# A decoder layer: the soft mask on VectorE, fill matmuls, four column blocks in cross attention, and expert rows added in DRAM by the scatter

## The reference

```
x = x + attn(layernorm(x))       # 16 heads of 128, in 8 segments of 64 tokens, over 2 batches of 512
x = x + xattn(layernorm(x), ctx) # 16 heads of 16, causal, keys and values from ctx_512
x = x + experts(layernorm(x))    # top 2 of 8 experts
```

## Time and profile before

| | us |
|---|---|
| median of 3 runs | 564.37 |
| the runs | 564.37, 571.93, 560.82 |
| the profiled execution, its own time | 561.27 |
| its span, first to last instruction | 559.5 |
| TensorE busy | 491.8 (88%) |
| VectorE busy | 339.7 (61%) |
| ScalarE busy | 323.3 (58%) |
| POOL busy | 144.0 (26%) |

### The profile page before, as it was taken

How to read it: one execution, slowest core, us unless ns; L and a number is a source line. 1 busy time by engine, 2 the same in 40 slices (tenths; PEclk the granted TensorE clock), 3 DMA queues, 4 the chain that set the end, 5 groups by cost and what they waited for, 6 DMA issues and landing times. The chain is left out here.

```text
span 559.5 us, 11805 instructions
## 1 busy us (share of the span) xinstructions
PE 491.8 (88%) x4163; PEld 419.0 (75%) x4164; DVE 339.7 (61%) x749; ACT 323.3 (58%) x762; POOL 144.0 (26%) x141
## 2 busy tenths in 40 slices
PE   2989999999899999999989799998507999999960
PEld 1778888888898888888689677776405888888850
DVE  5376666666725666666566376666652666666654
ACT  4477777788416777777662388887203444444430
POOL 5110000013000000000000438998011455555530
PEclk9999999999899999999999899999857999999995
DMA  9411111111100112110000033442221344444527
GB/s 264 160 59 57 56 56 56 56 57 57 39 1 20 57 57 56 56 56 0 1 1 2 2 101 127 147 131 102 76 94 51 119 169 156 151 159 158 165 76 225
DMA packets 24001, 48.05 MB, mean 86 GB/s; under 512 B 2960, under 2 KB 11168, under 8 KB 23968
## 3 DMA queue, kind: packets, MB, share of 16 engines
q1 hardware_dynamic: 21120, 41.17, 22.9%
q0 software_dynamic: 2240, 6.04, 3.1%
q10 hardware_dynamic: 608, 0.39, 0.3%
HBM read 42.48 MB, written 5.11 MB: 85 GB/s over the span
## 5 line engine op out<-in xcount | busy, mean ns | idle before, releaser
L651 PE MATMUL psum<-a_xt_hi,a_qk_hi 128*128 128x512 f32 x128 | 54.8, 428 | 1.4 <-DVE a_xt_lo L508 1.4
L570 DVE COPY a_weights_t<-psum 64x256 f32<-64x256 f32 x32 | 13.7, 428 | 63.5 <-PE psum L766 63.5
L1391 POOL DMA_INDIRECT picks_dram<-x_wout,e_pick_row x23 | 38.7, 1683 | 52.3 <-DVE x_wout L1554 52.3
L651 PE MATMUL psum<-a_xt_lo,a_qk_hi 128*128 128x512 f32 x128 | 51.7, 404 | 0.0
L651 PE MATMUL psum<-a_xt_hi,a_qk_lo 128*128 128x512 f32 x128 | 50.8, 397 | 0.0
L967 ACT ACTIVATE x_probs<-psum,x_neg_max 128x128 f32<-128x128 f32 x128 | 45.3, 375 | 8.1 <-DVE x_neg_max L1024 8.1
L1432 ACT ACTIVATE e_inner_hi<-psum 128x512 fp32r<-128x512 f32 x23 | 13.7, 598 | 57.9 <-PE psum L1614 57.9
L896 POOL MEMSET x_mask<- 128x512 bf16 x1 | 0.5, 524 | 172.3 <-POOLq L248 172.3
L1605 PE MATMUL psum<-expert_w_hi,e_x_hi 128*128 x92 | 39.2, 426 | 2.2 <-DVE e_x_lo L1532 2.2
L936 POOL TENSOR_TENSOR expert_w_lo<-x_xn_t,expert_w_hi 128x1024 fp32r<-128x1024 f32 x16 | 37.7, 2355 | 1.3
L780 PE MATMUL psum<-a_weights_t,a_v 64*128 64x64 f32 x256 | 34.9, 276 | 3.4 <-issue 2.5
(11 more groups left out here) (232 smaller groups left out, 1486.3 us busy)
## 6 DMA issues: line engine op xcount, KB each, us to landing
x_k_t<-in_expert_wo SPq DMA_DIRECT2D x23, 512.0 KB
a_qk_raw<-in_wqk SPq DMA_DIRECT2D x32, 256.0 KB, 2.6
x_xn_t<-in_expert_w SPq DMA_DIRECT2D x16, 512.0 KB, 3.8
a_wv_raw<-in_wv SPq DMA_DIRECT2D x17, 256.0 KB, 2.8
x_sb<-in_x SPq DMA_DIRECT2D x2, 512.0 KB, 5.1
x_k_t<-in_wo SPq DMA_DIRECT2D x1, 1024.0 KB, 10.5
x_v<-in_wo SPq DMA_DIRECT2D x1, 1024.0 KB, 13.1
xn_dram<-xn SPq DMA_DIRECT2D x1, 1024.0 KB, 4.4
```

The costliest lines, as they stand in the source:

```text
L570: dve.tensor_copy(weights_t[SEG:P, :, 0:2, :], t_ps[SEG:P, :, 0:2, :]).then_inc(wt_ready, 1)
L651: last = pe.matmul(out, pick_l(left[a], k), pick_r(right[b], k), start=start and n == 0, stop=n == 3 * KD - 1, skip_group_check=not start)
L1391: pool.indirect_dma_start(out=picks_dram, out_offset=bass.IndirectOffsetOnAxis(ap=pick_row[:, tile:tile + 1], axis=0), in_=y_rows[:, slot, ...
```

## The change

In attention:

- The mask is mixed once, into PSUM bank 3, and VectorE copies it to SBUF (`mask_f`). Per head the mask matmul goes; VectorE adds the mask to the scores (one operation more) and takes the maximum from SBUF.
- TensorE gets fill matmuls, whose results nobody reads, of 128x512 in fp32: four before the first transposes, eight behind them, and four in expert_phase while it waits for the first gather. The first transposes go sequence by sequence, each when its own xn is ready.
- The queries and keys of head 17 are made ahead of `output(0)`, and two of the eight cross products ahead of `output(1)`.

In cross attention `weigh` runs once per sequence with 16 matmuls, ordered so that four blocks of 32 partitions come in turn.

In the experts `sums_dram` holds one row per token and begins as a copy of x. The scatter adds into it (`compute_op=ALU.add`); each scatter waits until the one before has landed. So the share must be in y before: 48 small matmuls bring each row's share to its partition (`row_share`), and the copy of y multiplies with it. The tail is four DMAs from `sums_dram` to the output. VectorE's loop over the tiles is unrolled.

```diff
@@ attention
+            dve.wait_ge(mask_mixed, 1)
+            dve.tensor_copy(mask_f[:, :], c.bank[3][:, 0:HB * SEG])
...
-                dve.tensor_reduce(row_max[:, :, :], soft_ps, AX.X, ALU.max).then_inc(max_ready, 1)
+                dve.tensor_tensor(shifted[:, :, :, :].rearrange("p j g t -> p (j g t)"), c.bank[2][:, 0:HB * SEG], mask_f[:, :],
+                                  ALU.add).then_inc(masked_ready, 1)
+                dve.wait_ge(masked_ready, s.n + 1)
+                dve.tensor_reduce(row_max[:, :, :], shifted[:, :, :, :], AX.X, ALU.max).then_inc(max_ready, 1)
...
+            def keep_busy(times):
+                filled = sigma[:, :, :, :].rearrange("p a b t -> p (a b t)")
+                for _ in range(times):
+                    pe.matmul(c.bank[2][:, :], filled[:, 0:P], filled[:, 0:BANK], start=True, stop=True)
...
-                pe.matmul(c.bank[2][:, 0:HB * SEG], mixed_b[:, :], mask[:, :, :], start=True, stop=False,
-                          skip_group_check=True)
...
+            pe.wait_ge(fills_ready, 1)
+            keep_busy(4)
             pe.wait_ge(consts_ready, 6)
-            pe.wait_ge(fills_ready, 1)
+            pe.matmul(c.bank[3][:, 0:HB * SEG], mixed_b[:, :], mask[:, :, :], start=True, stop=True).then_inc(mask_mixed, 1)
             transpose_x(0)
+            keep_busy(8)
...
                 if not s.at(HALVES - 1, H - 1):
                     linear_scores(s.n + 1)
+                if s.at(0, H - 1):
+                    project(s.n + 2, 1, s.member, True)
+                elif s.at(HALVES - 1, H - 1):
+                    cross_products(range(6, 8))
                 if s.at(s.half, H - 1):
                     output(s.half)
@@ cross attention
-                for place, group, k, odd in across_groups(ch):
-                    head = k * CH + group * 2 + odd
-                    last = pe.matmul(ht_ps[group * ROWG:(group + 1) * ROWG, k, :],
-                                     v_pad[:, b % 2, head, :], probs_t[:, ch, place, :],
-                                     start=odd == 0, stop=odd == 1)
+                for k in range(KD):
+                    for odd in range(2):
+                        for group in range(4):
+                            last = pe.matmul(ht_ps[group * ROWG:(group + 1) * ROWG, k, :], v_pad[:, b % 2, k * CH + group * 2 + odd, :],
+                                             probs_t[:, group // 2, (group % 2) * 4 + k * 2 + odd, :], start=odd == 0, stop=odd == 1)
@@ experts
+            sp.dma_start(sums_dram[0:B * P, :].rearrange("(b p) d -> p b d", p=P), c.x_sb[:, :, :]).then_inc(sums_begun, 16)
+            sp.dma_start(sums_dram[B * P:(B + 1) * P, :], c.x_sb[:, 0, :]).then_inc(sums_begun, 16)
...
-            for b in range(B):
-                for k in range(TOPK):
-                    sp.dma_start(picked[k][:, b, :], picks[:, k, b, :]).then_inc(gathered[b], 16)
-            for b in range(B):
-                sp.wait_ge(mixed, TOPK * (b - b % 2) + 3 + b % 2)
-                sp.dma_start(out[b], c.x_sb[:, b, :]).then_inc(out_stored, 16)
+            for b in range(0, B, 2):
+                sp.dma_start(out[b:b + 2].rearrange("b p d -> (b p) d"), sums_dram[b * P:(b + 2) * P, :]).then_inc(out_stored, 16)
...
                 pool.wait_ge(y_ready, tile + 1)
-                pool.indirect_dma_start(out=picks_dram, out_offset=bass.IndirectOffsetOnAxis(ap=pick_row[:, tile:tile + 1], axis=0),
-                                        in_=y_rows[:, slot, :], in_offset=None).then_inc(y_stored[slot], 16)
+                if tile > 0:
+                    pool.wait_ge(y_stored[1 - slot], 16 * ((tile + 1) // 2))
+                pool.indirect_dma_start(out=sums_dram, out_offset=bass.IndirectOffsetOnAxis(ap=sum_row[:, tile:tile + 1], axis=0),
+                                        in_=y_rows[:, slot, :], in_offset=None, compute_op=ALU.add).then_inc(y_stored[slot], 16)
...
-                dve.tensor_copy(y_rows[:, slot, :], y_ps[slot]).then_inc(y_ready, 1)
+                dve.tensor_scalar(y_rows[:, slot, :], y_ps[slot], row_share[:, tile:tile + 1], None, ALU.mult).then_inc(y_ready, 1)
...
             pe.wait_ge(owner_known, 1)
+            for _ in range(4):
+                pe.matmul(c.bank[7][:, :], c.ident[:, :], c.x_sb[:, 0:2, :], start=True, stop=True)
             pe.wait_ge(picks_known, 1)
...
             columns(1, 1, 0, False)
+            pe.wait_ge(in_share_ready, 1)
+            for n in range(PICKS):
+                for part in range(3):
+                    last = pe.matmul(share_ps, row_hot[:, n, :], in_share[:, n, part, :],
+                                     start=n == 0 and part == 0, stop=n == PICKS - 1 and part == 2)
+            last.then_inc(row_share_done, 1)
```

148 lines of the change are left out of this document (79 added, 69 removed).

## The result

| | before | after |
|---|---|---|
| median | 565.5 (4 runs, 560.82 to 571.93) | 569.54 (4 runs, 568.93 to 575.0) |
| profiled execution / its span | 561.27 / 559.5 | 568.93 / 567.1 |
| ratio after / before | | 1.0137, 95% interval 1.0087 to 1.0188 |

The kernel became slower by 0.9 to 1.9%. The forecast was 549, faster by 2.2%; 569.5 lies in the upper part of its range, but on the wrong side of "no change".

A forecast was written before the change was run, and what follows sets the result against it. It took each stage to have its own bound (ScalarE's copy at heads, TensorE among expert tiles, DMA in the tail). Sum: 561.3 + 2.3 + 0 - 2.3 - 1.7 - 5.2 - 2.2 + 2 - 5.5 = 548.7, said 549; range 540 to 572.

The forecast's parts named there:

- the stores: Experts: each adding scatter waits for the landing before, interval 4.95 instead of 4.86 over 22 intervals, +2 us.
- rival (a): Experts, POOL's wait before each store: adding stores become the bound; chance 0.20 above 5.5 us apart, 0.16 above 6.0.
- L: Experts: time from one adding store's issue to the next's, put at 3.14 + 1.54 + 0.27 = 4.95 us.
- sign of being wrong: Experts or heads: store interval above 5.5, or the head's copy of the transposed weights waiting for VectorE.
- The next load, which has 4 us of slack: Experts, POOL: the load of tile+2 queues behind the store's wait and was said to have 4 us of slack.
- Cross attention: -5.2: Cross attention: weighing once instead of twice saves 0.65 us in each of eight batches, -5.2; ends -4 and -7.
- Fills at the start: +2.3: Start of attention: eight fills delay the first product, which then runs at full clock; +2.3 us, from -0.5 to +5.
- The mask: Attention heads: VectorE's added operation is narrowly covered by ScalarE's wait; 0 us in all, from -3 to +3.
- The half change: Between attention halves: head 17's product fills TensorE's wait; -1.5 from order and -0.8 from the clock, -2.3 us.
- The end of attention: Before the output of half 1: two cross products fill TensorE's wait of 2.27; -1.7 us, from 0 to -1.7.
- the fills in the prologue: Start of the experts: four fills during the gather wait raise the clock for tile 0; -2.2 us, chance three in four.
- the tail: End of the kernel: four DRAM-to-DRAM copies replace sixteen loads and the mixes; -5.5 us, from -4 to -7.

The follow-up runs named there:

- the two sum buffers: Kernel before with the experts' part of the change alone, but adding scatters alternate between two buffers without waiting for the one before: 569.14, ratio 1.012.
- the combined kernel: Kernel before plus new order, single weigh with five fills, prologue fills, mask on TensorE, plain scatters and a tail of eight 256 KB loads: 553.87, ratio 0.9837.

## Why the prediction was wrong

**The step that failed: the stores, "+2".** The mechanism was in the forecast as rival (a), with the right place and break-even: L = 5.5 breaks even against the other terms, and L came out at 5.52. Inside L the landing was right (4.68 forecast, 4.75 measured), the hand-over was not: "POOL has such a gap too behind the landing, an estimate of 0.27" took TensorE's issue gaps of 0.20 to 0.33 for POOL's gap behind a landing, which is 0.77. 0.5 x 22 = 11 of the 12.6 missed are this, and the landing's 0.07 x 22 = 1.5 the rest. The forecast stood 0.09 above the interval it had to fit under, so any error in L was multiplied by 22. The forecast's own sign of being wrong, an interval above 5.5, is what came.

That the landing came out right is in part luck. It was put together from an issue beside VectorE (1.71) and a reading priced by one gather, whose 4.24 was long for this stage (those behind it land in 3.4 to 3.9) and ends at the landing, so that the 0.3 for TensorE's start had no place in it. In the chain POOL issues away from VectorE's operation, in 1.59, and the landing follows 3.16 later, where 2.97 was forecast. Beside that operation, as the forecast had it, an adding store's issue takes 2.31 and its landing 6.0 to 6.6 (the two sum buffers).

**"The next load, which has 4 us of slack"** was wrong as well, though in the chained kernel it did not decide. In the kernel before TensorE already waited for the gather at 5 of the tiles from 440 to 540 (1.4 in all), so there was no slack; with two buffers a gather delayed by 0.6 on POOL held it at 16 (8.6).

**"Cross attention: -5.2"** was right for the sequences: a period fell by 0.70, for 0.65 taken, and the -4.5 in the table are the seven periods between the first and the last spread. The column blocks overlap fully: the rule of the Trainium skill ("TensorE: Matmul & The Clock Gate", Part 3: Packing small matmuls, section The mechanism) that a weight load overlaps running matmuls only when the row group differs, which would have had -4, is not borne out by the 1.08 for thirty-two records. The limit was not the one named. ScalarE's waits for the maximum, which should be gone, are still 6.7 of 8.1. Between the first and the last spread TensorE's busy time fell from 56.3 to 49.2, 1.0 per period, and it now waits 2.9 in all for ScalarE's exponentials, for 0.3 before. (The 0.20 behind a go was also counted twice, in the 0.53 and in the 1.0.) What failed is that I let the stage end with its last sequence. In the stretch behind it the faster stage met POOL, whose work has its own pace, and TensorE, less busy than before, lost its clock: +6.2.

**"Fills at the start: +2.3"** came out at +1.9, but fills and mask share it: taken away from the changed kernel the fills give back 1.0, and 0.9 stay, which are the mask's and which I had at 0. **The mask** over the other heads is 0.03 to 0.04 per head less in most steps and 0.45 more in three, together within the ends; in those three the cover was not there. **The half change** (-2.6 for -2.3) has the right sum from parts that were not: the clock, low from 144.1 to 147.5 before and not at all now, gives 1.7 instead of 0.8, and the order 0.9 instead of 1.5. **The end of attention** (-2.2 for -1.7), **the fills in the prologue** (-2.8 for -2.2) and **the tail** (-6.5 for -5.5) were right in mechanism and size.

**The clock drop between heads 1 and 2** (2.9 of the +3.4) was in no case of mine. It stays open what lets it come.

So the rest without the stores was worth 14.6 - 7.6 = 7.0 and not 14.6. The stretch behind cross attention took 6.2 of the difference and the heads 1 and 2 took 3.4; the terms that came out better than forecast gave about 2 back.

## What to carry to other kernels

Before making a stage shorter, look at what runs beside its end at its own pace (here POOL's last split at 388 to 391), and at what TensorE has left to do there: a collision that lay 1 us away cost 1.9, a clock at half behind a TensorE that was less busy 4 more, and the stage had gained 4.5. A chain of DMAs, one behind the other's landing, is priced by landing plus the waiting engine's own gap after a landing, taken from a row of that engine; and where it comes within a tenth of the interval that it must fit, its error is multiplied by the number of links. Taking a bound away (two buffers) needs the next one priced first: here POOL's way to the gather, behind the issue of the adding store.

## What the runs showed of the hardware

- POOL starts its next indirect DMA 0.73 to 0.77 behind the landing that it waited for, with an adding store as with a plain one; behind VectorE's signal 0.28. SP goes on 0.02 behind a landing, ScalarE 0.03 (the combined kernel).
- An adding scatter of 128 KB lands 4.75 after the start of its issue in the chain (median), 3.7 to 3.9 in the last three stores, and 6.0 to 6.6 when it is issued next to VectorE's operation; a plain one lands in 2.40 by itself and 3.15 next to that operation. The issue takes 1.55 by itself and 2.31 next to VectorE's operation, against 0.97 and 1.71.
- Sixteen plain fp32 matmuls of 32 columns, in four column blocks in turn, take 1.08; eight in two blocks take 1.07.
- A VectorE operation of 128x256 in SBUF that takes 0.41 took 2.35 when POOL's subtraction of 128x1024 (2.34) had just begun; the three behind it took 0.40 to 0.41.
- TensorE's clock can fall to half, or not, behind the same work at the same times: with the mask on VectorE it fell between heads 1 and 2 in 4 of 7 profiles, with the mask on TensorE in 1 of 6.
